# Two adaLN transformer layers on one core: rows of q and k by element, then head, with loads and the gates' chain moved

## The chip, the cores and the metric

The kernel runs on one core of one Trainium2 chip. The time is the device time of one execution in microseconds (us), the median over several runs. A profiled execution of the kernel before gives the trace. PE is TensorE, DVE is VectorE, ACT is ScalarE, POOL is GpSimd and SP is SyncE; PEld is TensorE's weight load.

## The reference

Two layers on x of 2048 rows by 128, float32. Each modulates a layer norm, adds gated attention, modulates a second layer norm and adds a gated mixture of experts.

```python
mod = (_silu(L0_c) @ L0_wmod).reshape(L0_c.shape[0], 6, 1, -1)
sa, ca, ga, sb, cb, gb = (mod[:, 0], mod[:, 1], mod[:, 2], mod[:, 3], mod[:, 4], mod[:, 5])
ga = (2 * (ga >= 0) - 1) * jnp.maximum(jnp.abs(ga), 0.25)
gb = (2 * (gb >= 0) - 1) * jnp.maximum(jnp.abs(gb), 0.25)
h = _layernorm(x, axis=-1) * (1 + ca) + sa
x = x + ga * _L0_attn_ref(h, ...)
h = _layernorm(x, axis=-1) * (1 + cb) + sb
x = x + gb * _L0_ffn_ref(h, ...)
```

The first attention has 16 heads of 8 elements. q is h @ W_q; a latent of 32, normalised, gives k and v; q and k get rotary position codes over halves of 4 elements, `[x1 * cos - x2 * sin, x1 * sin + x2 * cos]`; then causal softmax over all 2048 rows, and W_o. The second layer's attention makes q, k and v from each head's own 8 elements by 8x8 weights, without rotary codes; x is one sequence of 2048 rows for both. The experts (8, top 2) are not touched by the change.

## The kernel before

Everything stays on one core. `open_first` makes the first layer's q, k and v, `attention(.., 0)` uses them, `route` and the experts follow, `open_second` makes q, k and v of the second layer, `attention(.., 1)` uses them. Each of these is a block: one list of instructions per engine, written out by hand with semaphores, and a block begins on every engine when all engines have ended the one before.

**Three parts and 8 elements per row.** TensorE multiplies q and k as bf16, so each float32 value is split into three bf16 parts (hi, mid, lo), `m.parts[i][:, a, t]`, i = 0 for q and 1 for k. A head has only 8 elements; the score matmul takes 72 = 3 x 24 partitions, all pairs of parts, and 8 more (96 to 103, from `SHIFT0`) for the shift by the row's maximum. To bring parts of four heads (a group, `GH`) from the 128 rows of `parts` into that shape they go through DRAM: `store` (L715) writes a stretch of columns of q or k, `load_q` (L727, nine DMAs a call) and `load_k` (L736, three DMAs) read it back into `QS` and `KS`, which have two buffers. Group 0 is loaded by SP in pieces: columns 0 to 511 (chunk 0), 512 to 1023 (chunk 1) and the second half. Groups 1 to 3 are loaded whole by POOL (`load_group`: zeros to the shift rows at L720, nine loads of q, three of k). Before, row (head, element, part) of `q_parts` lies next to the other parts of its element, and a `load_q` DMA writes 8 partitions that are three apart.

**The first opening.** DVE, ACT and POOL go over eight steps n: q of chunks 0 to 3, then k of chunks 0 to 3. `rope(n)` on DVE multiplies by cos (L391) and sin (L392) and adds (L397) to `qf`; ACT casts the hi part (L333); `residue(n)` on DVE subtracts it (L404); ACT casts the mid part (L338); POOL subtracts again and writes the lo part (L495, semaphore `lo_done`). SP waits for `lo_done` and stores. At DVE's start stand two copies of `sbc` (L416), at its end the chain of the gates: `rows_out` is waited for, then five passes over 128x512 and two over 128x128 (L471 to L482) make sign(g) * max(|g|, 0.25) and scale `m.wo`.

**The attention.** Work comes in 16 units (group, 512 query rows). A table, `ORDER`, made by the function `schedule`, fixes TensorE's order: tiles of row maxima (L870), which DVE reduces (L964, L966), then the unit's "turn" (L875), a transposition of the split shift; DVE copies it to `shrow` (L980), SP sends it to the shift rows of `QS` (L813), and only then the unit's score matmuls (L901), exponentials on ACT (L946) and products with v (L917) can run. TensorE takes all of this in one order, so a wait for a shift holds the tiles behind it. Unit 0 is (0, 0), unit 1 (0, 1), unit 2 (0, 2), unit 3 the first of group 1. Two tiles of unit 1 stand ahead of unit 0's turn. In the block of the first attention POOL copies v, fills the shift part of the second buffers (L833), loads ones (L835) and then calls `load_group` for group 1; `load_group` of group g waits until group g - 2 is through. SP's list begins with the wait for the last store (`stored2`) and the loads of the second half, and its shifts come after.

**The second opening** has the same splitting without rotary codes; steps go q, k of chunk 0, q, k of chunk 1 and so on; the lo part is L705.

## Time and profile before

| | |
|---|---|
| median of 3 runs | 1486.29 us (1485.65 to 1486.48) |
| profiled execution | 1486.3 us, span of its instructions 1484.4 us |
| PE busy | 1215.6 us (82%) |
| DVE busy | 938.0 us (63%) |
| ACT busy | 696.8 us (47%) |
| POOL busy | 231.5 us (16%) |
| slices of 37 us at 90% PE or more | 25 of 40, 22 of them in the two attentions |
| DMA | 63.99 MB, mean 43 GB/s |

The busy time tells which engine works most, not what a wait is worth. The page has the costliest groups with the idle time ahead of them; the timeline shows each engine's instructions in order, with the idle time before one in brackets and what ended it. A DMA's issue is an instruction of the queue (SPq, or POOL) and has its own duration; the landing is given apart, as a median over the DMAs of a window.

### The profile page before, as it was taken

What the parts mean: (1) busy time and instruction counts of PE and PEld (TensorE: products, weight loads), DVE (VectorE), ACT (ScalarE), POOL (GpSimd) and SP (SyncE); (2) the same over time, 40 slices, a digit from 0 to 9 for tenths busy, and PEclk for the clock granted to TensorE, in tenths of its full rate; (3) what the DMA queues carried; (4) which work ended last, traced back from release to release, by engine and by line L of the source; (5) the groups of instructions that cost most, each with busy time, mean ns of one, the idle gap of its engine ahead of it and who ended that gap; (6) DMA issues with size and microseconds to landing.
All of it is one profiled execution on the core that took longest, in us unless ns stands there. A gap on an engine that the chain in (4) does not pass through costs nothing. (4 is left out here: it accounts for less than half of the span.)

```text
span 1484.4 us, 21009 instructions
## 1 busy us (share of the span) xinstructions
PE 1215.6 (82%) x7346; PEld 526.9 (35%) x7347; DVE 938.0 (63%) x2574; ACT 696.8 (47%) x928; POOL 231.5 (16%) x336
## 2 busy tenths in 40 slices
PE   6568999999999995079353899999999999585994
PEld 4322333323333334047121233332333334444663
DVE  6668888888788744001442888888878874442443
ACT  4313546666566673033321354666656667321331
POOL 2240000202000000725140000020200000063442
PEclk9668999999999996579655999999999999688997
DMA  3370100404020000121255011050400000011113
GB/s 127 103 118 3 31 16 16 83 16 84 16 74 3 3 2 1 52 63 50 89 127 69 2 62 32 31 84 3 69 2 2 3 3 2 1 42 41 49 48 105
DMA packets 47342, 63.99 MB, mean 43 GB/s; under 512 B 8529, under 2 KB 35569, under 8 KB 46913
## 3 DMA queue, kind: packets, MB, share of 16 engines
q1 hardware_dynamic: 35504, 38.75, 9.1%
q0 software_dynamic: 11744, 24.01, 8.8%
q8 instruction: 57, 0.93, 0.3%
q14 instruction: 37, 0.30, 0.1%
HBM read 45.42 MB, written 18.92 MB: 43 GB/s over the span
## 5 line engine op out<-in xcount | busy, mean ns | idle before, releaser
L946 ACT ACTIVATE probs_at<-st 128x1024 f32<-128x1024 f32 (+3 forms) x640 | 544.8, 895 | 367.2 <-PE st L901 240.6
L964 DVE TENSOR_REDUCE mxp_at<-mx 128x1 f32<-128x512 f32 x768 | 497.8, 685 | 113.6 <-PE mx L870 112.9
L870 PE MATMUL mx<-ks,qs 128*128 128x512 bf16 (+3 forms) x1280 | 382.6, 370 | 46.6 <-PEq L585 13.5
L901 PE MATMUL st<-qs,ks 128*128 128x512 bf16 (+3 forms) x1280 | 356.7, 356 | 32.3 <-DMA qs<-shrow_at 31.5
L917 PE MATMUL av<-probs_at,vs 128*32 128x512 f32 (+3 forms) x2560 | 301.4, 543 | 0.2
L966 DVE CUSTOM_DVE_ANT_0 junk_at<-mx,maskN 128x384 f32<-128x384 f32 (+3 forms) x512 | 241.1, 485 | 87.4 <-PE mx L870 85.5
L870 PEld LDWEIGHTS mx<-ks,qs 128*128 128x128 bf16 x1280 | 105.5, 99 | 402.3 <-DVE mxp_at L964 186.7
L901 PEld LDWEIGHTS st<-qs,ks 128*128 128x128 bf16 x1280 | 123.7, 99 | 132.3 <-DMA qs<-shrow_at 32.7
L1181 POOL DMA_INDIRECT perm<-rows,pos x64 | 63.1, 985 | 489.5 <-SPq L1290 238.7
L904 PE MATMUL st<-maskTb,identb 128*128 128x128 bf16 x512 | 100.3, 221 | 0.0
L917 PEld LDWEIGHTS av<-probs_at,vs 128*32 128x32 f32 x2560 | 50.7, 108 | 108.5 <-issue 97.3
L720 POOL DMA_DIRECT2D qs<-in_zrow_dram x6 | 3.5, 588 | 521.9 <-PE av L917 521.6
L1515 DVE TENSOR_TENSOR hid_f<-st,sg_f 128x352 f32<-128x352 f32 x39 | 20.5, 525 | 73.0 <-ACT sg_f L1496 73.0
L904 PEld LDWEIGHTS st<-maskTb,identb 128*128 128x128 bf16 x512 | 50.7, 99 | 17.4 <-issue 0.3
L1274 DVE SCALAR_TENSOR_TENSOR eo_f<-mx,rows_f,gates 128x128 f32<-128x128 f32 x16 | 4.5, 344 | 79.2 <-PE mx L1247 79.2
L1408 POOL DMA_INDIRECT eo<-eo_f,slot_f x39 | 38.5, 986 | 61.9 <-DMA eo<-eo_f,slot_f 34.1
L1229 PE MATMUL st<-pack_sb,rows_f 128*128 128x128 f32 x32 | 5.3, 293 | 51.0 <-DMA rows_f<-perm 51.0
L946 ACT ACT_TABLE_LOAD x2 | 2.6, 1283 | 86.2 <-PE st L904 86.2
L966 DVE DVE_READ_ACCUMULATOR2_ANT mxp_at<- 128x1 f32 x512 | 42.5, 83 | 0.0
L1496 ACT ACTIVATE sg_f<-st 128x352 f32<-128x352 f32 x39 | 18.1, 464 | 48.4 <-PE st L1442 48.4
L1441 PE MATMUL st<-weights,hTt_f 128*128 x78 | 34.0, 519 | 8.1 <-ACT hTt_f L1490 5.4
L1490 ACT ACTIVATE hTt_f<-mx,modc 128x128 f32<-128x128 f32 x39 | 17.8, 458 | 41.4 <-PE mx L1436 41.4
(241 smaller groups left out, 1059.7 us busy)
## 6 DMA issues: line engine op xcount, KB each, us to landing
qs<-q_parts POOLq DMA_DIRECT2D x54, 128.0 KB, 6.3
ks<-k_parts POOLq DMA_DIRECT2D x18, 384.0 KB, 12.0
weights<-in_w_dram SPq DMA_DIRECT2D x16, 256.0 KB, 3.0
perm<-in_pad_dram SPq DMA_DIRECT2D x1, 2600.0 KB, 10.8
rows_f<-perm SPq DMA_DIRECT2D x39, 65.0 KB, 1.8
q_parts<-weights SPq DMA_DIRECT2D x3, 768.0 KB, 3.8
rows_f<-perm SPq DMA_DIRECT2D x8, 260.0 KB, 2.9
got_pj<-eo SPq DMA_DIRECT2D x4, 512.0 KB, 7.2
```

The costliest lines, as they stand in the source:

```text
L870: pe.matmul(buf[:, 0:w], QS[p][:, j, (4 * Q + qb) * P:(4 * Q + qb + 1) * P], KS[p][:, j, c * CH:c * CH + w], start=True, stop=True).then_i ...
L901: mm = pe.matmul(st[half][:, y, off:CH], KS[p][:, j, kb * P:(kb + 1) * P], QS[p][:, j, Q * CH + off:(Q + 1) * CH], start=True, stop=True, ...
L904: mm = pe.matmul(st[half][:, y, off:off + P], m.identb[:], m.maskTb[:], start=False, stop=True, skip_group_check=True)
L917: mm = pe.matmul(avb[32 * j:32 * j + 32, off:CH], VS[p][:, kb, j, :], probs[:, s % 2, j, off:CH], start=kb == 0, stop=kb == TPC * Q + 3, t ...
L946: act.activation(probs[:, s % 2, 2 * half:2 * half + 2, off:CH], st[half][:, :, off:CH], ACT.Exp, scale=SCALE).then_inc(exp_done[half], 1)
L964: ins = v.tensor_reduce(dst, buf[:, 0:w], AX.X, ALU.max)
L966: ins = v.tensor_tensor_reduce(junk[:, k % MXBUF, 0:w], buf[:, 0:w], m.maskN[:, CH - w:], 1.0, -3e38, ALU.add, ALU.max, dst)
L1181: g.indirect_dma_start(out=dram[f"perm{L}"], out_offset=bass.IndirectOffsetOnAxis(ap=m.pos[:, i, b:b + 1], axis=0), in_=m.rows[:, i, b], i ...
L1408: g.indirect_dma_start(out=dram["eo1"], out_offset=bass.IndirectOffsetOnAxis(ap=slot[z][:, 0:1], axis=0), in_=eo[z][:], in_offset=None).th ...
L1441: pe.matmul(G[z % 2][:, 0:FF1], hT[z % 2][:], gw[:, bass.ds(e, 1), :], start=True, stop=True)
L1496: act.activation(sg[z % 2][:], G[z % 2][:, 0:FF1], ACT.Silu).then_inc(silu_done, 1)
L1515: v.tensor_tensor(hid[z % 2][:], U[z % 2][:, 0:FF1], sg[z % 2][:], ALU.mult).then_inc(hid_ready, 1)
```

## The change

1. Weights, tables and rows go by element, then head: partition e * 16 + h instead of h * 8 + e, in both layers' q and k. The rotated weights become plain halves. `q_parts` and `k_parts` hold three planes of 128 rows, one a part. A `load_q` DMA now writes 8 neighbouring partitions, and the four heads of a row lie next to each other in DRAM, so that a whole group's row is one run of 16 KB. cos and sin are full 128-row tables in DRAM.
2. SP's lists: in the first opening q's chunks 0 and 1 are stored and loaded one at a time as soon as they are there; in both layers the loads of chunk 1 (k alone in the first, q and k in the second) move from the opening's block into the attention's.
3. In the first opening the adds of the odd steps move from DVE to POOL (`add_turned`), with two buffers `tmp`; the copies of `sbc` move behind the other weights; the value matmuls use four banks.
4. The gates' chain moves from the opening to the first attention, on DVE just ahead of the copy of unit 2's turn (`finish_gates`); the matmuls with `m.wo` wait for it.
5. POOL waits for `shift_set[0]`, the landing of the first unit's shift, before it loads group 1, in both layers.

```diff
+        def add_turned(eng, n):
+            eng.wait_ge(cos_done, n + 1)
+            eng.wait_ge(proj_used, n + 1)
+            if n >= 2:
+                eng.wait_ge(r_done, n - 1)
+                eng.wait_ge(hi_done, n - 1)
+            eng.tensor_tensor(qf[n % 2][:], tmp[n % 2][:, 0], tmp[n % 2][:, 1], ALU.add).then_inc(qf_ready[n % 2], 1)
...
-                for z, n in enumerate((1, 3)):
-                    sp.wait_ge(lo_done, n + 1)
-                    store(sp, m, 0, dram, 0, slice((n - 1) * CH, (n + 1) * CH), m.sem(f"q_stored{z}"))
-                sp.wait_ge(m.sem("q_stored0"), 16)
-                load_q(sp, m, 0, dram, 0, cols(0), m.sem("first_in0"))
                 for c in range(2):
-                    sp.wait_ge(lo_done, NC4 + c + 1)
-                    store(sp, m, 0, dram, 1, cols(c), m.sem(f"stored{c}"))
-                    sp.wait_ge(m.sem(f"stored{c}"), 16)
-                    load_k(sp, m, 0, dram, 0, cols(c), m.sem(f"first_in{c}"))
-                    if c == 0:
-                        load_q(sp, m, 0, dram, 0, cols(1), m.sem("first_in1"))
-                        sp.wait_ge(m.sem("q_stored1"), 16)
-                    else:
-                        load_q(sp, m, 0, dram, 0, slice(T // 2, T), m.sem("first_in2"))
+                    sp.wait_ge(lo_done, c + 1)
+                    store(sp, m, 0, dram, 0, cols(c), m.sem(f"q_stored{c}"))
+                    sp.wait_ge(m.sem(f"q_stored{c}"), 16)
+                    load_q(sp, m, 0, dram, 0, cols(c), m.sem(f"first_in{c}"))
+                sp.wait_ge(lo_done, NC4)
+                store(sp, m, 0, dram, 0, slice(T // 2, T), m.sem("q_stored2"))
+                sp.wait_ge(lo_done, NC4 + 1)
+                store(sp, m, 0, dram, 1, cols(0), m.sem("stored0"))
+                sp.wait_ge(m.sem("stored0"), 16)
+                load_k(sp, m, 0, dram, 0, cols(0), m.sem("first_in0"))
+                sp.wait_ge(lo_done, NC4 + 2)
+                store(sp, m, 0, dram, 1, cols(1), m.sem("stored1"))
+                sp.wait_ge(m.sem("q_stored2"), 16)
+                load_q(sp, m, 0, dram, 0, slice(T // 2, T), m.sem("first_in2"))
                 sp.wait_ge(lo_done, NS)
                 store(sp, m, 0, dram, 1, slice(T // 2, T), m.sem("stored2"))
...
-                pe.wait_ge(rows_out, 1)
                 for c in range(NC4):
+                    if c == NC4 - 1:
+                        pe.wait_ge(rows_out, 1)
                     values(c)
...
                 def rope(n):
                     i, c = steps[n]
-                    if n:
-                        v.wait_ge(qf_ready, n)
                     if n >= 2:
-                        v.wait_ge(r_done, n - 1)
+                        v.wait_ge(qf_ready[n % 2], n // 2)
                     v.wait_ge(proj_ready, n + 1)
-                    v.tensor_tensor(tmp[0][:], product(n), cosT[:, cols(c)], ALU.mult).then_inc(chain.sem, 1)
-                    v.tensor_tensor(tmp[1][:], rotated(n), sinT[:, cols(c)], ALU.mult).then_inc(proj_used, 1)
-                    v.wait_ge(chain.sem, chain.next())
-                    v.wait_ge(proj_used, n + 1)
-                    if n >= 2:
-                        v.wait_ge(hi_done, n - 1)
-                    v.tensor_tensor(qf[n % 2][:], tmp[0][:], tmp[1][:], ALU.add).then_inc(qf_ready, 1)
+                    v.tensor_tensor(tmp[n % 2][:, 0], product(n), cosT[:, cols(c)], ALU.mult).then_inc(cos_done, 1)
+                    v.tensor_tensor(tmp[n % 2][:, 1], rotated(n), sinT[:, cols(c)], ALU.mult).then_inc(proj_used, 1)
+                    if n % 2 == 0:
+                        add_turned(v, n)
...
-                v.wait_ge(silu_done, 1)
-                for l in range(2):
-                    v.tensor_copy(sbc[:, l, :], scol[:, l:l + 1].to_broadcast([P, P])).then_inc(bc_done, 1)
...
+                for n in range(NS + 1):
+                    if n < NS and n % 2:
+                        add_turned(g, n)
+                    if n:
+                        i, c = steps[n - 1]
+                        g.wait_ge(mid_done, n)
+                        g.tensor_tensor(parts[i][:, 2, cols(c)], res[(n - 1) % 2][:], parts[i][:, 1, cols(c)], ALU.subtract).then_inc(lo_done, 1)
...
-                    sp.wait_ge(m.sem(f"stored{c}"), 16 * 3)
-                    load_q(sp, m, 1, dram, 0, cols(c), m.sem(f"first_in{c}"))
-                    load_k(sp, m, 1, dram, 0, cols(c), m.sem(f"first_in{c}"))
+                    if c == 0:
+                        sp.wait_ge(m.sem("stored0"), 16 * 3)
+                        load_q(sp, m, 1, dram, 0, cols(0), m.sem("first_in0"))
+                        load_k(sp, m, 1, dram, 0, cols(0), m.sem("first_in0"))
...
-    dst = bass.AP(dram[f"{('q_parts', 'k_parts')[i]}{L}"].tensor, cols.start, [[3 * T, P], [T, 3], [1, cols.stop - cols.start]])
+    dst = bass.AP(dram[f"{('q_parts', 'k_parts')[i]}{L}"].tensor, cols.start, [[T, P], [P * T, 3], [1, cols.stop - cols.start]])
...
-            eng.dma_start(m.QS[g % 2][3 * a * HD + b:3 * (a + 1) * HD:3, :, cols], bass.AP(
-                dram[f"q_parts{L}"].tensor, (g * GH * HD * 3 + a) * T + cols.start,
-                [[3 * T, HD], [3 * HD * T, GH], [1, cols.stop - cols.start]])).then_inc(done, 16)
+            r = (3 * a + b) * HD
+            eng.dma_start(m.QS[g % 2][r:r + HD, :, cols], bass.AP(
+                dram[f"q_parts{L}"].tensor, (a * P + g * GH) * T + cols.start,
+                [[H * T, HD], [T, GH], [1, cols.stop - cols.start]])).then_inc(done, 16)
...
-            dram[f"k_parts{L}"].tensor, g * GH * 3 * HD * T + cols.start,
-            [[T, 3 * HD], [3 * HD * T, GH], [1, cols.stop - cols.start]])).then_inc(done, 16)
+            dram[f"k_parts{L}"].tensor, g * GH * T + cols.start,
+            [[H * T, 3 * HD], [T, GH], [1, cols.stop - cols.start]])).then_inc(done, 16)
...
-                sp.wait_ge(s_("stored2"), 16 * (1 + 2 * L))
-                if L:
-                    load_q(sp, m, L, dram, 0, slice(T // 2, T), first_in[2])
-                load_k(sp, m, L, dram, 0, slice(T // 2, T), first_in[2])
+                for z, part in ((1, slice(CH, 2 * CH)), (2, slice(T // 2, T))):
+                    sp.wait_ge(s_(f"stored{z}"), 16 * (1 + 2 * L))
+                    if L:
+                        load_q(sp, m, L, dram, 0, part, first_in[z])
+                    load_k(sp, m, L, dram, 0, part, first_in[z])
...
+                g.wait_ge(shift_set[0], 16 * (L * (NU // 4) + 1))
                 load_group(g, m, L, dram, 1, kq_loaded[1])
...
+                        pe.wait_ge(wo_ready, 2)
...
+                def finish_gates():
+                    g2, s2 = m.gates[:].rearrange("p a d -> p (a d)"), junk[:, 0]
+                    v.tensor_scalar(s2, g2, 0., 2., ALU.is_ge, ALU.mult).then_inc(gates.sem, 1)
+                    v.wait_ge(gates.sem, gates.next())
+                    v.tensor_scalar(s2, s2, -1., None, ALU.add).then_inc(gates.sem, 1)
+                    v.wait_ge(gates.sem, gates.next())
+                    v.tensor_tensor(g2, g2, s2, ALU.mult).then_inc(gates.sem, 1)
+                    v.wait_ge(gates.sem, gates.next())
+                    v.tensor_scalar(g2, g2, .25, None, ALU.max).then_inc(gates.sem, 1)
+                    v.wait_ge(gates.sem, gates.next())
+                    v.tensor_tensor(g2, g2, s2, ALU.mult).then_inc(gates.sem, 1)
+                    v.wait_ge(gates.sem, gates.next())
+                    for l in range(2):
+                        v.tensor_tensor(m.wo[l], m.wo[l], m.gates[:, 2 * l], ALU.mult).then_inc(wo_ready, 1)
...
+                    if L == 0 and (kind, x) == ("turn", 2):
+                        finish_gates()
...
+    by_row = lambda t: np.tile(np.repeat(t.astype(np.float32), H, 0), (2, 1))
+    by_element = lambda w: w.reshape(-1, H, HD).transpose(0, 2, 1).reshape(-1, P)
```

SP in the first opening and at the start of the first attention. Names: `q_parts` is the store (L715 before, L708 now) and the source of `load_q` (L727, L721); `qs` and `ks` are `QS` and `KS`. Before:

```order
L715 DMA q_parts<-weights 384x1x1024 x2
L727 DMA qs<-q_parts 8x4x512 x9
L715 DMA k_parts<-weights 384x1x512
L736 DMA ks<-k_parts 24x4x512 x3
L727 DMA qs<-q_parts 8x4x512 x9
...
L727 DMA qs<-q_parts 8x4x1024 x9
L715 DMA k_parts<-weights 384x1x1024
L210 UNCONDITIONAL_BRANCH
```

Now, up to the first shift:

```order
L708 DMA q_parts<-weights 128x3x512
L721 DMA qs<-q_parts 8x4x512 x9
...
L708 DMA q_parts<-weights 128x3x1024
L708 DMA k_parts<-weights 128x3x512
L730 DMA ks<-k_parts 24x4x512 x3
L708 DMA k_parts<-weights 128x3x512
L721 DMA qs<-q_parts 8x4x1024 x9
L708 DMA k_parts<-weights 128x3x1024
L221 UNCONDITIONAL_BRANCH
...
L730 DMA ks<-k_parts 24x4x512 x3
L730 DMA ks<-k_parts 24x4x1024 x3
L808 DMA qs<-shrow_at 8x4x512 x3
```

The first store is half as long and has the first nine loads behind it, a second pair of the same follows, and three k loads are behind the block's end.

SP in the second layer, from the stores of chunk 1 (opening) to the first shift (attention), now:

```order
L708 DMA q_parts<-weights 128x3x1024
L708 DMA k_parts<-weights 128x3x1024
L577 UNCONDITIONAL_BRANCH
L794 UNCONDITIONAL_BRANCH
L721 DMA qs<-q_parts 8x4x512 x9
L730 DMA ks<-k_parts 24x4x512 x3
L721 DMA qs<-q_parts 8x4x1024 x9
L730 DMA ks<-k_parts 24x4x1024 x3
L808 DMA qs<-shrow_at 8x4x512 x3
```

Twelve loads, those of chunk 1, stood ahead of these two stores before; 24 loads stand between the block's start and the first shift now, where 12 stood.

DVE in the first attention, around the copy of unit 2's turn (L980 before, L994 now), now:

```order
L985 TENSOR_REDUCE mx_at<-mxp_at 128x16
L988 CAST nsh_at<-mx_at 128x16
L990 TENSOR_TENSOR nsh_at<-mx_at,nsh_at 128x16
L978 TENSOR_REDUCE mxp_at<-mx 128x1
...
L955 TENSOR_SCALAR junk_at<-gates 128x512
L957 TENSOR_SCALAR junk_at<-junk_at 128x512
L959 TENSOR_TENSOR gates<-gates,junk_at 128x512
L961 TENSOR_SCALAR gates<-gates 128x512
L963 TENSOR_TENSOR gates<-gates,junk_at 128x512
L966 TENSOR_TENSOR pack_sb<-pack_sb,gates 128x128 x2
L994 COPY shrow_at<-mx 8x512
```

The six rows from L955 to L966 stood at the end of the first opening.

## Rows read from the trace of the kernel before

**Rows 1.** Costliest groups: busy us, mean ns, idle before and what ended it.

```profile
L901 PE MATMUL st<-qs,ks 128*128 128x512 bf16 (+3 forms) x1280 | 356.7, 356 | 32.3 <-DMA qs<-shrow_at 31.5
```

**Rows 2.** Timeline of SP, first opening: start, us, engine, line, what.

```profile
41.88 6.61 SPq L715 DMA_DIRECT2D q_parts<-weights  x2
...
55.55 0.55 SPq L715 DMA_DIRECT2D k_parts<-weights  x1
58.39 1.16 SPq L736 DMA_DIRECT2D ks<-k_parts  x3
...
70.01 6.26 SPq L727 DMA_DIRECT2D qs<-q_parts  x9
76.32 0.55 SPq L715 DMA_DIRECT2D k_parts<-weights  x1
```

**Rows 3.** Timeline of all engines, start of the first attention.

```profile
77.86 0.48 PE L870 MATMUL mx<-ks,qs 128*128 128x128 bf16 x3 [13.12 <-DVEq L955]
...
85.23 2.66 DVE L974 CAST nsh_at<-mx_at 128x16 bf16<-128x16 f32 x1
...
89.28 0.10 PEld L870 LDWEIGHTS mx<-ks,qs 128*128 128x128 bf16 x1 [0.22 <-issue]
...
89.87 0.78 SPq L813 DMA_DIRECT2D qs<-shrow_at  x1
...
97.73 0.10 PEld L901 LDWEIGHTS st<-qs,ks 128*128 128x128 bf16 x1 [5.02 <-DMA qs<-shrow_at]
```

**Rows 4.** The same, shift and first scores of unit 1.

```profile
115.11 0.71 SPq L813 DMA_DIRECT2D qs<-shrow_at  x1
...
117.78 1.06 PE L901 MATMUL st<-qs,ks 128*128 128x512 bf16 x2
```

**Rows 5.** The same, second opening's end, start of its attention.

```profile
751.86 1.15 POOL L705 TENSOR_TENSOR weights<-res_pj,weights 128x512 bf16<-128x512 f32 x1
...
763.81 0.48 PE L870 MATMUL mx<-ks,qs 128*128 128x128 bf16 x3 [13.46 <-PEq L585]
...
768.00 6.33 SPq L727 DMA_DIRECT2D qs<-q_parts  x9
...
768.94 0.66 POOL L720 DMA_DIRECT2D qs<-in_zrow_dram  x1 [0.30 <-POOL vs L825]
...
775.74 0.76 SPq L813 DMA_DIRECT2D qs<-shrow_at  x1
...
803.19 0.61 PE L901 MATMUL st<-qs,ks 128*128 128x512 bf16 x1 [26.74 <-DMA qs<-shrow_at]
```

**Rows 6.** Windows: length, PE, PEld, DVE, ACT, POOL, PEclk, DMA share, GB/s.

```profile
776.50:803.20 26.70, 0.01 (x1) 0.02 (x2) 0.78 (x3) 0.00 (x0) 0.29 (x1) 0.50 0.84 104
```

**Rows 7.** First opening: timeline; then DMA issues, us to landing.

```profile
5.62 2.35 DVE L416 COPY sbc<-scol 128x128 f32<-128x128 f32 x2 [5.62 <-ACT scol L350]
...
37.67 1.15 POOL L495 TENSOR_TENSOR weights<-res,weights 128x512 bf16<-128x512 f32 x1 [27.68 <-ACT weights L338]
...
x<-in_x_dram SPq DMA_DIRECT2D x4, 256.0 KB, 5.7
```

**Rows 8.** Timeline of DVE, gates' chain.

```profile
59.35 0.43 DVE L477 TENSOR_SCALAR ks<-ks 128x512 f32<-128x512 f32 x1
59.82 0.69 DVE L479 TENSOR_TENSOR gates<-ks 128x512 f32<-128x512 f32 x1
```

**Rows 9.** DMA issues at 88.8 to 89 us: KB each, us to landing.

```profile
ks<-in_zo_dram POOLq DMA_DIRECT2D x1, 128.0 KB, 4.7
qs<-in_zrow_dram POOLq DMA_DIRECT2D x1, 128.0 KB, 5.6
```

**Rows 10.** Group 3, first attention: DMA issues at 359.6; timeline of POOL, PE.

```profile
ks<-k_parts POOLq DMA_DIRECT2D x2, 384.0 KB, 11.6
...
353.62 4.86 POOL L727 DMA_DIRECT2D qs<-q_parts  x9
...
380.57 0.82 PE L870 MATMUL mx<-ks,qs 128*128 128x512 bf16 x3
```

More of the change, by code:

```diff
@@ L189, in open_first @@
         scol, sbc = sb("scol", [P, 2]), sb("sbc", [P, 2, P])
-        qf, res, tmp = ([sb(f"{k}{i}", [P, CH]) for i in range(2)] for k in ("qf", "res", "tmp"))
+        qf, res = ([sb(f"{k}{i}", [P, CH]) for i in range(2)] for k in ("qf", "res"))
+        tmp = [sb(f"tmp{i}", [P, 2, CH]) for i in range(2)]
         latn, latT = sb("latn", [P, TILES, LAT]), sb("latT", [LAT, T])
@@ L376, in _ @@
                         act.wait_ge(rows_ready, 1)
-                        act.copy(gate, bank[3]).then_inc(rows_out, 1)
+                        act.copy(m.gates[:].rearrange("p a d -> p (a d)"), bank[3]).then_inc(rows_out, 1)
                 mid(NS - 1)
```

59 lines of the change are left out of this document (21 added, 38 removed).

## The prediction

> **What bounds the kernel now.** I read the page first. Of TensorE's idle time before the first score matmul of a group (L901), 31.5 us hangs on one transfer, the shift rows [rows 1]. TensorE is busy nine tenths and more of nearly every slice once an attention is under way (the table above), so what is to be won lies where they start. There the timeline of SP's queue and the timeline of all engines give the order of events.
>
> In the first opening SP is the last to finish. Its first store is issued at 41.88 us, then it issues 27 loads of q in three batches of nine (the last in 6.26 us, 0.70 us each), k's in between, each behind stores it waits for, and its last store at 76.32 [rows 2]. TensorE idles 13.1 us and starts the first attention at 77.86, about 1.0 us after SP's last issue [rows 3]. Nothing but SP works in the last 11 us. The first shift DMA goes out at 89.87 and the scores start at 97.73, 7.86 us later; the shift of unit 1, with an empty queue, needs 115.11 to 117.78, that is 2.67 us [rows 3, 4]. The nine tiles TensorE has in hand meanwhile end at 93.0, so 4.7 us is bare wait.
>
> The second layer is worse. TensorE starts at 763.81, after 13.5 us idle, SP then issues the second half's loads from 768.00, comes to the shift only at 775.74, and the scores start at 803.19: 27.4 us later, 26.7 of them idle [rows 5]. In that stretch the DMA engines are 84% busy, 104 GB/s, and no engine computes [rows 6]: 2.8 MB, of which SP's last twelve loads are only 1.2. POOL began group 1's loads, 2.5 MB in 13 DMAs, at 768.94 [rows 5].
>
> The profiled span is 1484.4 us, its time 1486.3, equal to the median of the three runs (1486.29). I count against that.
>
> **The change, part by part.** *First opening.* (a) Two copies of `sbc` (2.35 us) leave the head of DVE's list; the statistics follow them at once. x lands 5.7 us after its issues (median), which begin at about 1.2 us [rows 7], so near 7.0, and 7.97 becomes 7.0: the chain moves up 0.9 us (between 0 and 2.35). The copies run later in a gap. (b) SP stores q chunk 0 as soon as its lo part is done. POOL's first lo ends at 38.82 [rows 7], less 0.9 is 37.9, against 41.88 now. From there by SP's own rows: a store of 384 KB and its landing 2.8 us (55.55 to 58.39), nine loads 6.3 to 7, so 47.5; store, landing, nine loads, so 56.7; two stores, about 4.6 us to the landing of the second behind 768 KB, three k loads 1.2, a store, nine loads 6.3 and a store: 70.5 where it was 76.9. Three k loads are gone into the next block. TensorE starts 6.3 us earlier, at 71.5. (c) The adds of the odd steps move to POOL (1.15 us for such a pass). DVE is past its last step before 59.35 [rows 8] and SP, whose last store follows its batch without a gap (70.01 + 6.26, then 76.32), needs the last lo part only at 70: nothing either way, under some 10 us of cover. The value matmuls, whose banks no longer wait, end 13 us before the block does, and count nothing too; nor do the contiguous weight and table rows. (d) The unit-1 tiles ahead of the first turn now need k loads that are issued after the block starts, at about 71.5 to 72.7; they are wanted 7.2 us later. Zero, with 1.5 us against it in the range.
>
> *First attention.* (e) POOL holds group 1's loads until the first shift has landed. The shift takes 2.7 us instead of 7.86, TensorE's tiles then end last: -4.7 us. With the cast at 85.23, which took 2.66 us beside POOL's fill of qs instead of 0.2, there may be 2.5 us more [rows 3]; I leave it in the range. (f) The gates' chain (five passes of 128x512 and two of 128x128) goes from idle DVE time to just before the copy of shift 2. A scalar pass takes 0.43 us with POOL quiet, a two-tensor pass 0.69 [rows 8], the last two have a quarter of the size, about 0.25 each by an estimate: 3 x 0.43 + 2 x 0.69 + 0.5 and small gaps, 3.3 us. Around there DVE has no gap and TensorE waits for it after each tile, so I charge +3.3 (0 to 3.5). (g) Held loads run into shift 1. They start with the scores and last 18 us at least (353.6 to 371, [rows 10]), and the shift of unit 1 goes out 17.4 us after the scores start. Delay between 0 and the 5.2 us that shift 0 has now; nearer 2, since only the tail is in flight: +2 in each layer.
>
> *Second opening.* (h) The loads of chunk 1 leave the block. The stores of the second half then go out when POOL's last lo parts are ready, at 751.9 and 753.0 [rows 5]; SP ends at about 753.7, TensorE starts at 754.5 instead of 763.8. SP issues 24 loads in the new block, 2 x 7.7 us: the shift goes out at 769.8, 5.9 us earlier. (i) How long does it lie behind SP's own loads, with POOL's gone? At least 2.7 us: scores at 772.5, -30.7. The other bound comes from eight neighbouring partitions, which each q load now writes (they were three apart). The two DMAs that already do this, ones and zeros into partitions 96 to 103, 256 KB together, are issued at 88.17 and 88.89 and landed 4.7 and 5.6 us later [rows 9], 6.4 us in all; less the 2.7 us that 32 KB takes it is 3.7 us for 224 KB, 61 GB/s. If every byte of the 1.73 MB behind the stores went at that rate from 757.9 on, scores would start near 789, -14. I take what lies between: q loads of 64 KB at 1.1 us each where SP issues one per 0.70, k loads, three times as many rows, 192 KB in the same 1.1. Then q and k of chunk 1 are through at 764, the half's q at 774, its k at 777, and the scores start at 779: -24.
>
> The Trainium skill speaks against this row order: SBUF — State Buffer, "Door 1: The DMA port swizzle", says that the bandwidth depends on how many of 16 ports the partitions reach, four neighbours sharing one of 27.2 GB/s; by it eight neighbours reach two ports, 54 GB/s, and the same sum would give 780.5 in place of 779. The trace nearly agrees, with 61 GB/s for eight neighbours.
>
> *Group loads.* (j) Their rows become one run of 16 KB where there were four of 4 KB; POOL's issue time (0.54 us each, [rows 10]) hardly moves. q loads alternate between halves of the DMA engines if two are in flight, so nine take 9/2 x 2.2 = 10 us where 1.2 MB now takes 8; +2 to +4 us per group. In the first layer group 3's last k loads are issued near 359.4 and land 11.6 us later, at 371; its first tile starts at 380.57 [rows 10], so they are hidden by 9 us.
>
> Sum: -6.3 - 4.7 + 3.3 + 2 - 24 + 2 = -27.7, 1486.3 - 27.7 = 1458.6; say **1459**.
>
> **The rivals.** *R1, cheap issue.* A q load costs SP 0.70 us, a k load, with three times the descriptors but neighbouring partitions, 1.16 / 3 = 0.39 [rows 2]. If the stride of three is what costs, 27 loads lose up to 0.3 us each; about 5.8 us of it reaches the start of the first scores (landings and the turn take over), and in the second layer the backlog hides it: 1453. Against it: the shift DMA also writes eight neighbours and takes 0.71 [rows 4]. *R2, no port limit.* The q loads drain as issued, (i) gives its better bound: -6.5, 1452. For it: 61 GB/s rests on two DMAs at once. *R3, dearer tails.* Shift 1 waits the full 5 us in each layer, with 16 KB pieces ahead of it, and the second layer's backlog is worth 5 us more: 1470. *R4, slower than before.* The held loads now go one by one at 61 GB/s: nine of 128 KB at 2.2 us is 20 us, k and zeros 10, so a group load takes 30 us instead of 18. The hidden margin of 9 us is exceeded by 3 us in two groups, shift 1 by 5 us twice: still 1472. Only from 37 us per load, where each of four later groups loses about 7 us beyond that, is the time over 1486; at 38 us it would be 1490. *R5, no effect of the hold.* SP's own queue, not POOL's loads, made the 27 us. Then (i) gives little: 9.3 from the earlier start shrinks to the 5.9 of the earlier issue, the first layer keeps its 7: about 1477. Against it: of the 2.8 MB that moved while the shift waited, SP's loads were under half.
>
> **How the numbers follow.** Forecast 0.40 (own range 1454 to 1464), R1 0.17, R2 0.13, R3 0.19, R5 0.05, R4 at 30 us per load 0.01, R4 with about 36 us 0.02 and with more 0.03. R1 and R2 together would be near 1447. The range 1446 to 1474 leaves out R5, R4 and some corners of the good side. A measurement of this kernel tells 0.2%, 3 us, from no change. Faster 0.95, within 0.2% 0.02, slower 0.03.
>
> **What would show it.** First tile of attention near 71.5 and the first scores near 87; in the second layer first tile near 754.5, shift issued near 770 and scores near 779. SP's nine q loads in 6.3 us for the forecast, in about 3.6 for R1. DVE's gates chain in one piece of 3.3 us ahead of shift 2. Shift 1 to scores 2.7 us if (g) is nothing, 8 for R3. TensorE waiting for DMA qs<-q_parts or ks<-k_parts at a group's first tile would be R4. I am wrong if the second layer's scores start after 790.

## The result, and the profile after

| | before | changed |
|---|---|---|
| median | 1486.38 us (1485.65 to 1486.53, 4 runs) | 1464.39 us (1462.93 to 1468.58, 4 runs) |
| ratio | | 0.9858, 95% interval 0.9836 to 0.9879 |
| profiled execution, span | 1486.3, 1484.4 us | 1468.6, 1466.7 us |
| TensorE busy | 1215.6 us | 1214.1 us |

The change makes the kernel 22 us faster, 1.4%. The forecast was 1459 us, the range 1446 to 1474. The profiled execution is the slowest of the four, 4.2 us above their median, so positions read from it understate the gain.

SP's timeline of the first opening, which answers to [rows 2]:

```profile
38.07 0.39 SPq L708 DMA_DIRECT2D q_parts<-weights  x1
40.97 3.06 SPq L721 DMA_DIRECT2D qs<-q_parts  x9
44.07 0.39 SPq L708 DMA_DIRECT2D q_parts<-weights  x1
46.61 3.02 SPq L721 DMA_DIRECT2D qs<-q_parts  x9
...
55.92 3.29 SPq L721 DMA_DIRECT2D qs<-q_parts  x9
59.25 0.38 SPq L708 DMA_DIRECT2D k_parts<-weights  x1
```

Nine loads of q cost 3.06 us of SP's time where they cost 6.26, and the last store is issued at 59.25, not 76.32. All engines at the start of the first attention, to be read beside [rows 3, 4]:

```profile
60.36 0.48 PE L866 MATMUL mx<-ks,qs 128*128 128x128 bf16 x3 [4.23 <-DVEq L952]
...
69.78 1.12 PE L866 MATMUL mx<-ks,qs 128*128 128x512 bf16 x3 [3.68 <-DMA ks<-k_parts]
...
72.25 0.87 SPq L808 DMA_DIRECT2D qs<-shrow_at  x1
...
75.17 0.63 PE L898 MATMUL st<-qs,ks 128*128 128x512 bf16 x1
...
77.25 0.65 POOL L713 DMA_DIRECT2D qs<-in_zrow_dram  x1
...
92.08 0.69 SPq L808 DMA_DIRECT2D qs<-shrow_at  x1
...
108.00 1.04 PE L898 MATMUL st<-qs,ks 128*128 128x512 bf16 x2 [13.04 <-DMA qs<-shrow_at]
...
142.21 0.29 PE L866 MATMUL mx<-ks,qs 128*128 128x128 bf16 x1 [3.01 <-DVEq L996]
```

The first tile starts 17.5 us earlier and the first scores (75.17) 22.6 us earlier. Then the shift of unit 1, issued at 92.08, needs 15.9 us to its scores, 13.0 of them idle; it needed 2.7 before [rows 4]. The row at 142.21 is TensorE waiting for DVE's gates chain. The second layer, beside [rows 5]:

```profile
747.07 0.33 PE L866 MATMUL mx<-ks,qs 128*128 128x128 bf16 x3 [4.14 <-PEq L577]
...
755.15 1.12 PE L866 MATMUL mx<-ks,qs 128*128 128x512 bf16 x3 [2.17 <-DMA ks<-k_parts]
...
757.62 0.75 SPq L808 DMA_DIRECT2D qs<-shrow_at  x1
...
765.95 0.61 PE L898 MATMUL st<-qs,ks 128*128 128x512 bf16 x1 [5.21 <-DMA qs<-shrow_at]
...
783.68 0.69 SPq L808 DMA_DIRECT2D qs<-shrow_at  x1
...
797.22 1.03 PE L898 MATMUL st<-qs,ks 128*128 128x512 bf16 x2 [10.63 <-DMA qs<-shrow_at]
```

Here 27.4 us from shift to scores became 8.3 for unit 0, but 2.7 became 13.5 for unit 1. Last, group 3's first tile in the second layer, which had no wait before (in the first layer, too, there is now one, of 1.7 us), and the DMA issues of a group load in the first attention, to be read beside [rows 10]:

```profile
1068.99 1.44 PE L866 MATMUL mx<-ks,qs 128*128 128x512 bf16 x3 [3.20 <-DMA ks<-k_parts]
...
qs<-q_parts POOLq DMA_DIRECT2D x9, 128.0 KB, 4.6
ks<-k_parts POOLq DMA_DIRECT2D x3, 384.0 KB, 22.2
```

Times from the start of the span, in us, of the same point in both profiled executions:

| point | before | changed | difference |
|---|---|---|---|
| first scores, first layer | 97.7 | 75.2 | -22.6 |
| scores of unit 1 | 117.8 | 108.0 | -9.8 |
| scores of unit 2 | 150.5 | 145.4 | -5.1 |
| last shift of the layer | 530.9 | 527.0 | -3.9 |
| first tile, second layer | 763.8 | 747.1 | -16.7 |
| first scores, second layer | 803.2 | 766.0 | -37.2 |
| scores of unit 1 | 823.8 | 797.2 | -26.6 |
| scores of unit 6 | 1000.9 | 977.0 | -23.9 |
| last shift of the layer | 1237.3 | 1218.5 | -18.8 |

Of the 56 us that the two openings and first shifts gained (22.6, and 33.3 from the end of the first layer's attention on), 37 were given back: 12.8 and 10.6 at the shifts of unit 1, the rest at the gates chain, behind late group loads and in stretches at a lower TensorE clock.

### The profile page after: what moved, and what is told of

The parts are those of the page before. It is cut to its first block and busy times, and to the rows that moved or that the text cites. A ratio compares the mean times of both kernels' runs of the same rounds, so it can differ in the third digit from the quotient of the medians.

```text
span 1466.7 us, 21010 instructions
## 1 busy us (share of the span) xinstructions
PE 1214.1 (83%) x7346; PEld 526.4 (36%) x7347; DVE 930.7 (63%) x2570; ACT 695.4 (47%) x928; POOL 235.3 (16%) x340
## 5 line engine op out<-in xcount | busy, mean ns | idle before, releaser
L898 PE MATMUL st<-qs,ks 128*128 128x512 bf16 (+3 forms) x1280 | 357.0, 356 | 32.7 <-DMA qs<-shrow_at 31.7
L980 DVE CUSTOM_DVE_ANT_0 junk_at<-mx,maskN 128x384 f32<-128x384 f32 (+3 forms) x512 | 241.4, 485 | 71.6 <-PE mx L866 69.7
L914 PEld LDWEIGHTS av<-probs_at,vs 128*32 128x32 f32 x2560 | 50.6, 108 | 108.0 <-issue 97.0
L1422 POOL DMA_INDIRECT eo<-eo_f,slot_f x39 | 38.2, 979 | 62.1 <-DMA eo<-eo_f,slot_f 33.6
L980 DVE DVE_READ_ACCUMULATOR2_ANT mxp_at<- 128x1 f32 x512 | 42.6, 83 | 0.1
L1233 POOL DMA_INDIRECT eo<-eo_f,slot_f x32 | 31.2, 976 | 36.4 <-DVE eo_f L1288 29.1
```

The costliest lines, as they stand in the source:

```text
L898: mm = pe.matmul(st[half][:, y, off:CH], KS[p][:, j, kb * P:(kb + 1) * P], QS[p][:, j, Q * CH + off:(Q + 1) * CH], start=True, stop=True, ...
L914: mm = pe.matmul(avb[32 * j:32 * j + 32, off:CH], VS[p][:, kb, j, :], probs[:, s % 2, j, off:CH], start=kb == 0, stop=kb == TPC * Q + 3, t ...
L980: ins = v.tensor_tensor_reduce(junk[:, k % MXBUF, 0:w], buf[:, 0:w], m.maskN[:, CH - w:], 1.0, -3e38, ALU.add, ALU.max, dst)
L1233: g.indirect_dma_start(out=dram["eo0"], out_offset=bass.IndirectOffsetOnAxis(ap=slot[e % 2][:, t4:t4 + 1], axis=0), in_=eo[e % 2][:, t4], ...
L1422: g.indirect_dma_start(out=dram["eo1"], out_offset=bass.IndirectOffsetOnAxis(ap=slot[z][:, 0:1], axis=0), in_=eo[z][:], in_offset=None).th ...
```

## The experiments

The kernels ran in four groups, each on one chip beside the kernel before, which took 1486.63 us in the first group, 1500.27 in the second (e4_before_hold, e6 to e8), 1485.26 in the third (f1, f3, f4) and 1484.36 in the fourth (e9_pitch). So ratios are compared, and places within one trace; a time that was expected stands on the scale of 1486, and goes with the ratio times 1486. The 14 us by which the second chip is slower lie behind the second attention: from the last shift to the end it is 260 us in its four traces and 247 to 248 in before, changed and e1_runs4k. Only the kernel before was run on more than one of these chips, so whether a ratio stays the same from chip to chip is not tested; f3_adds_dve below leaves room for a few tenths of a per cent.

### Group loads in 4 KB pieces (e1_runs4k)

```diff
+TR = T + 256
-    dst = bass.AP(..., cols.start, [[T, P], [P * T, 3], [1, cols.stop - cols.start]])
+    dst = bass.AP(..., cols.start, [[TR, P], [P * TR, 3], [1, cols.stop - cols.start]])
...
-                [[H * T, HD], [T, GH], [1, cols.stop - cols.start]])).then_inc(done, 16)
+                [[H * TR, HD], [TR, GH], [1, cols.stop - cols.start]])).then_inc(done, 16)
```

> The changed kernel with the rows of q_parts and k_parts in DRAM 4608 bytes apart instead of 4096 (a pad of 512 bytes), so that the four heads of a row are no longer one run: POOL's group loads move pieces of 4 KB, as in the kernel before, to the same neighbouring partitions, with the same DMAs in the same order. Theory A, long pieces: in the changed kernel an engine needs 2.0 us for a piece of 16 KB and the shift of unit 1 comes behind about five of them. With 4 KB pieces the shift of unit 1 takes at most 6 us from issue to scores in each layer (15.9 and 13.5 in the changed kernel), the waits at group 3's first tile (1.7 and 3.2 us) go, and the time is 1440 to 1450. Theory B, eight neighbouring partitions are the limit: nothing moves, 1461 to 1467, and the nine q loads still land about 2 us apart.

Measured: 1443.97 us (1441.67 to 1446.74), ratio 0.9716 (0.9697 to 0.9735): 20 us faster than the changed kernel. The waits at group 3 and at unit 6 are gone; the shift of unit 1 takes 5.8 us in the second layer, but still 9.6 in the first:

```profile
92.20 0.69 SPq L809 DMA_DIRECT2D qs<-shrow_at  x1
...
101.77 1.04 PE L899 MATMUL st<-qs,ks 128*128 128x512 bf16 x2 [6.66 <-DMA qs<-shrow_at]
```

Theory B, that piece size does nothing, falls. Theory A holds for the time, for the second layer and for the waits at group 3, but the first layer's 9.6 us is above its 6.

### Rows of q three apart again, pieces of 16 KB kept (e5_stride3)

```diff
-            eng.dma_start(m.QS[g % 2][r:r + HD, :, cols], bass.AP(
+            eng.dma_start(m.QS[g % 2][3 * a * HD + b:3 * (a + 1) * HD:3, :, cols], bass.AP(
```

> The changed kernel with each load of q writing eight partitions that are three apart again, everything else as changed. It leaves out the pairing of q's rows with k's: scores are products of other parts, the amount of work is the same. If the stride of three is what made SP's nine q loads cost 6.3 us (rival R1), they cost about 6.3 us again (3.1 in the changed kernel), first tile of the first attention 5 to 8 us later than 60.4, and POOL's group loads get shorter if neighbouring partitions are what slows them (shift of unit 1 under 10 us from issue to scores), the same if the 16 KB pieces are. If the stride is not the cause, 3.1 us and no change. Time by R1 with long pieces slow: 1466 to 1474.

Measured: 1452.06 us (1451.91 to 1452.34), ratio 0.9769 (0.9752 to 0.9787). A time of 1466 to 1474 was expected, slower than the changed kernel; it is 12 us faster.

```profile
40.64 6.41 SPq L721 DMA_DIRECT2D qs<-q_parts  x9
...
69.84 0.48 PE L866 MATMUL mx<-ks,qs 128*128 128x128 bf16 x3 [14.08 <-DVEq L952]
...
103.43 0.71 SPq L808 DMA_DIRECT2D qs<-shrow_at  x1
...
108.61 0.61 PE L898 MATMUL st<-qs,ks 128*128 128x512 bf16 x1 [2.27 <-DMA qs<-shrow_at]
...
qs<-q_parts POOLq DMA_DIRECT2D x9, 128.0 KB, 3.5
ks<-k_parts POOLq DMA_DIRECT2D x3, 384.0 KB, 11.7
```

SP's nine loads cost 6.41 us again and the first tile comes at 69.84, 9.5 us later than in the changed kernel (5 to 8 were expected): rival R1 is shown, the stride of three is what made issue dear. But a group load's k lands in 11.7 us in place of 22.2, with pieces of 16 KB in both, and the shift of unit 1 takes 5.2 us in place of 15.9. So the long piece is not enough either. From POOL's first issue to the end of the last piece, a group load took, over the six of each execution:

| | pieces of 4 KB | pieces of 16 KB |
|---|---|---|
| rows three apart | 17.0 to 21.4 (e4_before_hold) | 19.9 to 22.1 (e5_stride3) |
| neighbouring rows | 18.9 to 25.2 (e1_runs4k) | 28.4 to 32.8 (changed) |

It takes both to make 30 us. (The rows are q's; k's loads write 24 neighbouring partitions in all four. e4_before_hold, below, is the kernel before with one line added.) In these runs the row order thus gained 9.5 us at the first opening and lost more than that in the attentions.

### The distance of rows in DRAM alone (e9_pitch)

```diff
-    dst = bass.AP(..., cols.start, [[T, P], [P * T, 3], [1, cols.stop - cols.start]])
-    sp.dma_start(dst, m.parts[i][:, :, cols]).then_inc(done, 16)
+    for a in range(3):
+        dst = bass.AP(..., a * HD * EP + cols.start, [[EP, HD], [T, H], [1, cols.stop - cols.start]])
+        sp.dma_start(dst, m.parts[i][:, a, cols]).then_inc(done, 16)
```

> The pad of e1_runs4k changed two things at once: the length of the pieces and the distance of neighbouring partitions' rows in DRAM (64 KB before it, 72 KB with it). Here that distance alone changes: a pad of 4 KB behind each element's sixteen heads (68 KB apart), the four heads of a group still one run, so pieces of 16 KB. A store becomes three DMAs, one a part, which costs SP some 1 us per store in the openings. If the length of the pieces is the cause, as argued: group loads of 28 to 33 us as in the changed kernel, shift of unit 1 at 13 us or more, 1462 to 1470. If the distance of 64 KB is the cause: group loads of 20 to 25 us, the shift of unit 1 under 10 us, 1440 to 1455.

Measured: 1480.34 us (1475.62 to 1486.85) against 1484.36, ratio 0.9982 (0.9962 to 1.0002). The time missed both figures: the stores cost more than the 1 us each that I allowed, and the first tiles of the two attentions come 11 and 16 us later than in the changed kernel. What was asked is read from the group loads:

```profile
qs<-q_parts POOLq DMA_DIRECT2D x9, 128.0 KB, 4.9
ks<-k_parts POOLq DMA_DIRECT2D x3, 384.0 KB, 21.9
...
102.69 0.72 SPq L810 DMA_DIRECT2D qs<-shrow_at  x1
...
116.54 1.03 PE L900 MATMUL st<-qs,ks 128*128 128x512 bf16 x2 [10.97 <-DMA qs<-shrow_at]
```

All six take 27.3 to 31.7 us, k lands in 21.9, and the shift of unit 1 takes 13.9 and 14.2 us, as the theory of long pieces has it. The distance of 64 KB is not the cause. What is left is what the pad of e1_runs4k cuts: it makes four pieces of 4 KB of one of 16 KB. It also takes the rows off multiples of 4096 bytes in DRAM; no run has that alone, so the length itself is the likely cause and not the only one left.

### No hold (e2_no_hold)

```diff
-                g.wait_ge(shift_set[0], 16 * (L * (NU // 4) + 1))
```

> The changed kernel without POOL's wait for the first unit's shift. In the first layer POOL is busy with fills until 76.5 us and the shift has landed by 75.1, so nothing should move there. In the second layer the group loads start near 751.5 instead of 766.6. Theory A (the loads delay whatever shift is on its way): the shift of unit 0 waits about 10 us more, scores near 775 instead of 766, and the shift of unit 1, issued near 790, is quick (3 to 5 us): the wait only changes its place, 1460 to 1467. Rival: the hold is worth what the prediction gave it, the second layer starts its scores at 780 or later and nothing comes back: 1478 or more.

Measured: 1475.52 us (1474.72 to 1479.55), ratio 0.9924 (0.9907 to 0.9942), between the two figures: the theory's 1467 and its rival's 1478.

```profile
754.83 1.60 POOL L721 DMA_DIRECT2D qs<-q_parts  x3
...
763.13 0.75 SPq L808 DMA_DIRECT2D qs<-shrow_at  x1
...
794.85 0.61 PE L897 MATMUL st<-qs,ks 128*128 128x512 bf16 x1 [28.59 <-DMA qs<-shrow_at]
```

In the second layer the scores come at 794.85, not near 775: the first shift takes 31.7 us, that of unit 1 then only 2.7. The hold moves some 11 us of the wait to unit 1 and takes away the rest. In the first layer the first scores don't move (75.27 against 75.17): POOL is busy with its fills here too, and issues its first load of group 1 only at 74.93, 0.3 us ahead of those scores.

### Hold until the second unit's shift (e3_hold_second)

```diff
-                g.wait_ge(shift_set[0], 16 * (L * (NU // 4) + 1))
+                g.wait_ge(shift_set[1], 16 * (L * (NU // 4) + 1))
```

> The changed kernel with POOL waiting for the shift of unit 1 instead of that of unit 0 before it loads group 1. Theory A: both first shifts take 2.7 us, so the 13.0 and 10.6 us of waits at unit 1 go; the loads then run about 31 us from 95 and from 776, the first is hidden, the second reaches group 1's first tile at about 814 or a little before, costing 0 to 4 us there: 1440 to 1447. Rival: the collision moves on to the shift of unit 2, or group 1's first tile waits 10 us or more in both layers: 1458 or more.

Measured: 1442.6 us (1442.07 to 1450.4), ratio 0.9722 (0.969 to 0.9754). Shifts of unit 1 take 2.7 us in both layers, as theory A has it; group 1's first tile waits 1.8 us in the first layer and, in the second:

```profile
804.71 1.12 PE L866 MATMUL mx<-ks,qs 128*128 128x512 bf16 x3 [5.54 <-DMA ks<-k_parts]
```

That is 1.5 us more than the 4 expected.

### The hold alone in the kernel before (e4_before_hold), and with the second shift (f4_before_hold_second)

```diff
+                g.wait_ge(shift_set[0], 16 * (L * (NU // 4) + 1))
                 load_group(g, m, L, dram, 1, kq_loaded[1])
```

> The kernel before with the hold alone: POOL waits for the first unit's shift before it loads group 1, in both layers. Theory: the hold is worth some 15 us in the second layer with the old rows too, since the first shift then has only SP's own loads ahead of it; scores of the second layer near 785 instead of 803 (less 1 to 5 us for what the first layer gains), the first layer's 7.9 us from shift to scores becomes 2.9, and the shifts of unit 1, now beside 4 KB pieces, take 5 to 9 us instead of 2.7: 1468 to 1476. Rival R5 of the prediction, SP's own queue made the wait: 1482 or more.

Measured: 1475.84 us against 1500.27 for the kernel before on that chip, ratio 0.9842 (0.9825 to 0.9858).

```profile
773.13 0.76 SPq L813 DMA_DIRECT2D qs<-shrow_at  x1
...
778.02 0.61 PE L902 MATMUL st<-qs,ks 128*128 128x512 bf16 x1 [4.03 <-DMA qs<-shrow_at]
...
778.66 0.66 POOL L720 DMA_DIRECT2D qs<-in_zrow_dram  x1 [12.59 <-DMA qs<-shrow_at]
```

4.9 us from shift to scores in place of 27.4, where 2.7 to 2.9 is a shift with nothing ahead of it: with the old rows and twelve loads of SP's own ahead, nearly the whole wait was POOL's group load. R5 falls. Shifts of unit 1 take 5.8 and 3.6 us. By the ratio the time is 1463 us, better than the 1468 to 1476 expected. One line gives as much as the whole change (0.9858).

> The kernel before with one line added: POOL waits for the second unit's shift before it loads group 1, in both layers. e4_before_hold, with the wait for the first, gave a ratio of 0.9842, with the shifts of unit 1 still late (2.9 us idle in the first layer). Theory: those waits go as well, the loads of 17 to 24 us are through before group 1's first tile, 3 to 6 us less, ratio 0.980 to 0.982. Rival: group 1's first tiles wait, ratio 0.984 or more.

The index 0 in that line made 1. Measured: 1455.39 us against 1485.26, ratio 0.9811 (0.9795 to 0.9826), inside the theory's figures, and no first tile of a group waits. The interval lies below that of the whole change (0.9836 to 0.9879), and its last shift comes at 1205.6 in its trace, where the changed kernel has 1218.5 and the kernel before 1237.3. As far as ratios from two chips can tell, this one line, in the kernel before, gives more than all five parts of the change together.

### The chain of the gates back in the opening (e6_gates_opening)

```diff
                 residue(NS - 1)
+                v.wait_ge(rows_out, 1)
+                v.wait_ge(qf_ready[0], NS // 2)
+                g2, s2 = m.gates[:].rearrange("p a d -> p (a d)"), tmp[0][:, 0]
+                v.tensor_scalar(s2, g2, 0., 2., ALU.is_ge, ALU.mult).then_inc(gates.sem, 1)
...
-                    if L == 0 and (kind, x) == ("turn", 2):
-                        finish_gates()
```

> The changed kernel with the chain of the gates back at the end of DVE's list in the first opening, where DVE stands idle for 5.7 us. Theory: the 3.3 us chain there costs nothing, and the 3.0 us that TensorE waited ahead of the shift of unit 2 come back: 1459 to 1463, and from unit 2 to unit 3 of the first layer no wait over 1 us. Rival: the opening's block ends later by the chain (DVE's first tile work at 60.7 slips by 1 us or more) or the 3 us return as a longer wait elsewhere: 1463 to 1467.

Measured: 1474.75 us, ratio 0.9843 (0.9818 to 0.9869), 2 us better than 0.9858 and inside both intervals; e7_chunk1_back, on the same chip with the chain in the attention, has 0.9841. So no gain in time is shown. The trace tells more: TensorE's wait of 3.0 us ahead of the shift of unit 2 is gone (its tiles follow with gaps under 0.8), and the chain has its price in the opening, 5.1 us beside POOL's work, with a first tile at 62.5. In e7_chunk1_back that is 61.0. So 1.5 of the 3 us are paid back there; in e8_both, below, the first tile came at 60.7 with the chain in the same place, so even this is not certain.

```profile
56.37 1.38 DVE L476 TENSOR_SCALAR tmp<-gates 128x512 f32<-128x512 f32 x1
...
60.99 0.49 DVE L487 TENSOR_TENSOR pack_sb<-pack_sb,gates 128x128 f32<-128x128 f32 x2
...
62.82 0.29 DVE L980 CUSTOM_DVE_ANT_0 junk_at<-mx,maskN 128x128 f32<-128x128 f32 x1 [1.34 <-PE mx L883]
```

### Chunk 1's loads back in the second opening (e7_chunk1_back)

```diff
-                    if c == 0:
-                        sp.wait_ge(m.sem("stored0"), 16 * 3)
-                        load_q(sp, m, 1, dram, 0, cols(0), m.sem("first_in0"))
...
+                    sp.wait_ge(m.sem(f"stored{c}"), 16 * 3)
+                    load_q(sp, m, 1, dram, 0, cols(c), m.sem(f"first_in{c}"))
```

> The changed kernel with the second layer's loads of chunk 1 back in the opening's block, right behind chunk 1's stores. The prediction gave the move of these loads 9.3 us of earlier start (h). Theory: with q loads at 0.34 us each the twelve loads cost SP 4.3 us in a stretch where it waits for the last lo parts anyway; first tile of the second attention at most 3 us later than 747.1, the wait of 2.2 us for k's chunk 1 goes, and the first scores come within 2 us of 766.0: 1461 to 1467, the move is worth nothing by itself. Rival, as predicted: 5 us or more later, 1468 or above.

Measured: 1475.89 us, ratio 0.9841 (0.9821 to 0.9862), no slower than the change.

```profile
739.62 3.03 SPq L720 DMA_DIRECT2D qs<-q_parts  x9
742.69 1.13 SPq L729 DMA_DIRECT2D ks<-k_parts  x3
...
745.68 0.48 PE L865 MATMUL mx<-ks,qs 128*128 128x128 bf16 x3 [6.56 <-PEq L577]
...
755.20 0.75 SPq L807 DMA_DIRECT2D qs<-shrow_at  x1
...
762.50 0.61 PE L897 MATMUL st<-qs,ks 128*128 128x512 bf16 x1 [4.17 <-DMA qs<-shrow_at]
```

From the first layer's last shift (523.5) to the first tile it is 222.2 us; in nine other traces on the changed kernel, with the loads moved and a store as one DMA, this was 220.1 to 222.9, in three of the old kernel's order (before, e4, f4) 230.0 to 232.9. So these 10 us come without the move, with cheap issue (and stores of 0.36 to 0.49 us in place of 0.56 to 0.63); and e5_stride3, dear issue with the loads moved, has 221.8. Either is enough.

### Three edits together (e8_both), then SP's loads behind the shift (f1_half_after)

The pad of e1_runs4k, the wait of e3_hold_second and the chain's place of e6_gates_opening, each as in its diff above:

```diff
+TR = T + 256
...
+                v.wait_ge(rows_out, 1)
...
-                g.wait_ge(shift_set[0], 16 * (L * (NU // 4) + 1))
+                g.wait_ge(shift_set[1], 16 * (L * (NU // 4) + 1))
```

> The changed kernel with three edits: pieces of 4 KB (rows of DRAM padded), the hold until the second unit's shift, and the chain of the gates at the end of the first opening. Each alone took or should take a wait: if they add up, no wait for a shift of unit 1 (24 us in the changed kernel), none at a group's first tile, none ahead of unit 2's shift: 1428 to 1436. If the held loads of 20 to 24 us come too late for group 1 in the second layer, as with 16 KB pieces (5.5 us of wait), or the two cures cure the same wait, 1438 or more.

Measured: 1442.78 us against 1500.27, ratio 0.9615 (0.9597 to 0.9632). By the ratio that is 1429 us, inside the 1428 to 1436 expected if the three add up. No wait over 1 us at a shift of unit 1 or a group's first tile is left; the largest is the second layer's first shift, 10.0 us from issue to scores. For that one, SP's twelve loads of the second half were put behind it:

```diff
+                        if L and u == 0:
+                            load_part(2, slice(T // 2, T))
```

> e8_both with the second layer's loads of the second half (twelve DMAs, 1.2 MB) issued by SP behind the first unit's shift instead of ahead of it. In e8_both that shift took 10.0 us from issue to scores, TensorE idle 6.9 of them, behind SP's own loads. Theory (the backlog of SP's queue is the rest of the wait): about 3 us from issue to scores, no wait there, 5 to 7 us less than e8_both, ratio to the kernel before 0.956 to 0.959; the loads land some 10 us later, well before unit 2's first tile. Rival: unit 2's first tile or the shift of unit 1 (issued 27 us after the first) now waits for them and the time stays as e8_both, ratio 0.960 or more.

```profile
739.12 0.75 SPq L830 DMA_DIRECT2D qs<-shrow_at  x1
739.92 3.94 SPq L739 DMA_DIRECT2D qs<-q_parts  x9
...
743.90 1.14 SPq L748 DMA_DIRECT2D ks<-k_parts  x3
```

The scores follow at 742.04, 2.9 us behind the issue, and the shift of unit 1 comes 19.8 us behind the first's instead of 27.3. Measured: 1424.49 us (1422.49 to 1426.35) against 1485.26, ratio 0.9595 (0.9579 to 0.961), between the theory's 0.959 and the rival's 0.960. It is the fastest of all and beats both kernels: 4.1% below the kernel before. The step from e8_both is 3 us by the ratios, whose intervals overlap, and 5.8 us by the last shift in the two traces.

### The adds of the odd steps back on DVE (f3_adds_dve)

```diff
-                    if n % 2 == 0:
-                        add_turned(v, n)
+                    add_turned(v, n)
```

> e8_both with the adds of the odd steps in the first opening back on DVE (part c of the prediction, costed at nothing). If nothing hangs on them, as predicted: the first tile of the first attention within 1 us of 60.7 and the ratio to the kernel before within 0.002 of 0.9615. Rival: with SP's queue no longer the last to finish, DVE's list is now the bound of the opening and the adds cost 2 us or more there; or the other way, POOL's list is (an add and a subtraction of 1.15 us each per step), and the opening gets 1 us or more shorter.

Measured: 1433.65 us, ratio 0.9653 (0.9633 to 0.9673), 0.0038 above e8_both, outside the 0.002 expected. The first tile comes at 61.17 against 60.66 and the first layer's last shift 0.9 us later; the rest of the difference arises in the second layer, which this edit doesn't touch. So at most 1 us is shown, and why the ratio moved by some 5 us, on another chip than e8_both, stays open.

## Why the prediction was right, and where its steps failed

The median lies in the range, 5 us above the forecast, and that it is so near is luck: large errors went opposite ways. In the traces the two openings and first shifts gained 56 us where the sum has 35 (6.3, 4.7 and 24), and shifts of unit 1, gates and late loads gave back 37 where it has 7.3.

**(a), (b), the first opening: right in kind, too small.** TensorE's start was forecast at 71.5 and came at 60.4. The step that failed is "nine loads 6.3 to 7": three batches at 3.02 to 3.29 us save 9.4 of the 11.1 us. That was R1, given 0.17, and e5_stride3 shows it. (By its own terms the list in (b) adds up to 69.9, not 70.5.) The rows had both prices, 0.70 for rows three apart and 0.39 for neighbouring ones [rows 2]; I let the shift DMA's 0.71 speak against; it differs in its source, which is not DRAM, and what makes it dear no run shows. The price of R1 was wrong as well: "about 5.8 us of it reaches the first scores", where 75.17 against a forecast of about 87 is 12.

**(c), (d).** The adds cost nothing that can be shown. The loads of k's chunk 1 were late: TensorE waits 3.7 us at 69.78 and 2.2 in the second layer. I had put zero, with 1.5 in the range, and zero it is in the first layer: in e2_no_hold, with the same opening, that wait is 0.8 us and the first scores come at 75.27, no earlier. In the second it is about 1 us: e7_chunk1_back, without this wait, needs 9.5 us from the first tile to the shift, the changed kernel 10.6.

**(e), the first shift of the first layer: right time, wrong reason.** It took 2.9 us, but e2_no_hold has the same without the hold: with the opening 17 us shorter, POOL's fills keep its loads back until the shift is nearly through.

**(f), the gates' chain: right.** +3.3 forecast, 3.01 us of wait measured.

**(g), the collision with the shift of unit 1: the step that failed most.** "Nearer 2, since only the tail is in flight"; measured 13.0 and 10.6 us idle. The load was not at its tail, since it takes 30 us and not 18, and the scores are 17 us ahead of that shift. R3 had the place and 5 us; R4 had the length, "30 us instead of 18", but priced its collision at 5 us. (R4's way from 1472 at 30 us to 1486 at 37 us holds 7 us for two groups; with the four that it names it would be 1500. Nothing else hangs on it.)

**(h), (i), the second layer: direction right, size too small.** The first tile moved by 10 us against 9.3 forecast, if the traces are averaged; e7_chunk1_back shows that it comes without moving the loads. The 24 loads took SP 10.0 us, not 15.4. From shift to scores 8.3 us, where 9.2 was forecast. From the end of the first attention to these scores it was 33.3 us less, where 24 was forecast. The bound of 61 GB/s did not hold for SP's pieces of 1 and 2 KB, which went at a mean of 138 GB/s from 749 to 762 us; it came from two DMAs of POOL. That the hold ends the long wait was right, and e4_before_hold shows that POOL's load was nearly all of it. Of the 22 us that the whole change gains, the hold is worth 10 to 11 (e2_no_hold).

**(j), the group loads: failed.** "Hidden by 9 us" was 1.7 and 3.2 us of wait at group 3, and 2.7 at the shift of unit 6. TensorE's granted clock, 1.00 and 0.99 in the same tiles before, had a mean of 0.94 and 0.92 at these waits of 2.7 and 3.2 us, mostly 2.4 GHz with a stretch at 1.2. Before, then changed (length, PE, PEld, DVE, ACT, POOL, PEclk, DMA share, GB/s):

```profile
1000.90:1046.40 45.50, 44.91 (x285) 14.44 (x284) 38.09 (x101) 29.31 (x33) 0.00 (x0) 1.00 0.04 13
1057.10:1092.90 35.80, 34.03 (x216) 11.36 (x215) 28.19 (x65) 21.09 (x25) 7.70 (x14) 0.99 0.42 72
...
977.00:1025.10 48.10, 47.56 (x284) 15.25 (x285) 37.32 (x95) 29.59 (x33) 0.00 (x0) 0.94 0.02 3
1035.75:1075.00 39.25, 35.41 (x216) 11.54 (x215) 28.20 (x65) 21.09 (x25) 7.30 (x14) 0.92 0.48 65
```

The first stretch took 48.1 us where it took 45.5, which is 2.6 of the 8 us that were lost between unit 1 and the end of this layer; the second took 3.5 us more, 3.2 of them the wait itself.

**The row order and the ports.** From 96.7 to 102.4 us in the changed kernel eight pieces of 16 KB are in flight at a time, by their order mostly the last of q, half the DMA engines' time is unused, and a piece takes 2.02 us; that is 65 GB/s:

```profile
96.70:102.40 5.70, 0.00 (x0) 0.00 (x0) 0.00 (x0) 0.00 (x0) 0.00 (x0) 0.50 0.49 66
```

With rows three apart (e5_stride3, 92 to 96 us) such pieces took mostly 0.9 to 1.3 us. The Trainium skill, SBUF — State Buffer, "Door 1: The DMA port swizzle", was cited against this row order; by its rule eight neighbours reach two ports, an estimate of 54 GB/s. The trace agrees that long pieces into neighbours are slow, and its rate is a fifth above that estimate; the measurement decides. With 4 KB pieces in the same rows the load ran at 118 GB/s (e1_runs4k, 88 to 96 us):

```profile
88.00:96.00 8.00, 5.05 (x15) 1.42 (x15) 7.57 (x22) 0.00 (x0) 0.00 (x0) 0.65 1.06 118
```

That more DMAs with other rows are then in flight at once is argued, not tried.

## What to carry to other kernels

A bulk load that another queue starts at the same moment as a short transfer on the critical path can cost more than what stands in the transfer's own queue (here 23 us against 7): first hold it until the last such transfer before its own due time has landed, and put one's own later loads behind it too. When an order of rows or a layout is changed, count three things apart: what one issue costs, how long the pieces get, and how many partitions a DMA reaches; here cheap issue was given back by long pieces into few partitions, until a pad of 512 bytes per row cut the pieces, worth 20 us. Try the single parts of a change alone: here one line of it gave as much as the whole, and more with the second shift to wait for. After a change that brings the start forward, work out again which later transfers now meet.

## What the runs showed of the hardware

A DMA's issue on SP cost 0.70 us with eight destination rows three apart and 0.34 with eight neighbouring ones, with the same number and size of pieces; on POOL it was 0.52 to 0.54 either way. A short transfer does not share the engines piece by piece from its issue on: in the changed kernel the 32 pieces of the shift issued at 92.08 began only at 102.48 and were through at 105.7, while pieces of 16 KB of POOL's queue, 2.0 us each, went on being started ahead of them. With 16 KB pieces this wait was some five pieces long, then about one piece per turn. I had expected turns from the start. The Trainium skill, DMA: Bandwidth & Descriptors, section Queues, rings and completion order, says that an engine serves its queues in turn, a packet at a time; the trace agrees with turns after 102.5; a packet of several long pieces could make the first 10 us too, but no run here tried what sets the number of pieces ahead.
